# A second buffer for key and query parts, and a new order at the start of the first attention

## The chip, the cores and the metric

The kernel runs on one core of a Trainium2 chip. The metric is the device time in microseconds (us) of one execution, the median of several.

## What is computed

Two layers of cross-attention, each followed by a gated block, on `x` of shape (8, 256, 256) and a context `ctx_1024` of the same shape, in float32. The change touches the first of the four parts alone:

```python
# part 1: 16 heads of 16 columns; queries from the normed x, keys and values from the context
x = x + tanh(g_xattn[0]) * L0_xattn(_layernorm(x), ctx_1024, ctx_1024, Wq, bq, Wk, bk, Wv, bv, Wo, bo)
    # q = Q @ Wq + bq, k = K @ Wk + bk, v = V @ Wv + bv
    # out = softmax(q k^T / sqrt(16)) v, heads joined, @ Wo + bo
x = x + tanh(g_ffn[0]) * L0_ffn(_layernorm(x), ...)             # slots, routing, GRU
x = x + tanh(g_xattn[1]) * L1_xattn(ctx_1024, _layernorm(x), ...)  # 8 heads of 128
x = x + tanh(g_ffn[1]) * L1_ffn(x, ...)                         # quantized gate/up/down
```

## The kernel before

Each of the four parts is a function of its own with its own blocks of engine code, semaphores and a barrier at its end. `attention0` (line 91 on) is the first; a batch is one of 8 sequences of 256 positions. Each engine's instructions stand in the order in which the source issues them, and an engine executes its own list in that order; waits on semaphores tie the lists together. SP and, in places, ScalarE and POOL issue DMAs.

Precision is kept by splitting: each of context, normed x, weights, keys and queries is held as a high part (float32r) and a low part (the rest). For a batch `n`, TensorE transposes context and normed x (`ctxT`, `xnT`, L587), ScalarE copies the high part (`ctxT_hi`, `xnT_hi`, L327, L332), VectorE the low part (`ctxT_lo`, `xnT_lo`, L461, L465). `project_k` and `project_q` (L606) are 12 matmuls each into PSUM; `k_high`/`q_high` (L342, ScalarE) and `k_low`/`q_low` (L471, VectorE) write the parts into `k_parts` and `q_parts`, of which there is one buffer. From there 24 DMAs of 64 KB a batch (`place`, L180) put the rows high, high, low (queries) beside high, low, high (keys) into `q_stack` and `k_stack`, which have two buffers, by the batch's parity (`par`). Each stack has two halves: steps 0 to 3 of a batch read half 0, steps 4 to 7 half 1. Semaphores `stack0` and `stack1` count the copies of a half.

A batch has 8 steps `r`, each for two heads. `scores(b, par, r)` (L645, 4 matmuls) makes scores from the stacks for the maxima, which VectorE takes in `pair_max` (L494, 2 instructions); POOL splits a pair of maxima (`split_max`), TensorE turns them (`turn_max`, L668) and ScalarE copies them (`shift_out`, L361). `shifted_scores` (L658, L661) makes the scores again, transposed, less the maximum, ScalarE takes the exponentials (L356), and `group` (L679) multiplies with the values. The scores run 4 steps ahead of the shifted scores, and batch `b + 2` is projected while batch `b` is attended to. Batches 0 and 1 are prepared ahead of the loop by code written out by hand, at the end of each engine's block:

- SP: after the loads, `first_stacks()` waits in turn for `k_hi`, `k_lo`, `q_hi` and `q_lo` of batch 0 and issues 6 key copies and 4 query copies for half 0 and 6 query copies for half 1; then `load_ctx(2)`, the load of x 2, and `stacks(1, 1, False)`.
- POOL: after its constants and `rstd_of(1)`, waits for `k_lo` and issues the 6 key copies of half 1 (L299, semaphore `first`); then `split_max(0, 0)`.
- ScalarE: `k_high(0)`, `xnT_hi(0)`, `ctxT_hi(1)`, the high part of Wv, `q_high(0)`, then waits for `q_lo` and issues the last 2 query copies of half 0, then `xnT_hi(1)`, tanh of the gates, `k_high(1)`, `q_high(1)`, `shift_out(0, 0)`.
- VectorE: ..., `q_low(0)`, `v_out(0)`, `xnT_lo(1)`, `k_low(1)`, two `pair_max`, `q_low(1)`, two `pair_max`.
- TensorE: ..., `xnT(1)`, `project_k(1)`, `scores(0,0,0)`, `project_q(1)`, `scores(0,0,1)` to `scores(0,0,3)`, `turn_max(0,0)`, and then the loop with `shifted_scores(0,0,0)` first.

`high` makes `k_high(n)` and `q_high(n)` wait until all copies of batch `n - 1` have landed, since they read the one buffer that it writes:

```python
act.wait_ge(s[projected], n + 1)
wait(act, s["stack0"], HALF * n)
wait(act, s["stack1"], HALF * n - HALF // 2)
if isinstance(n, int) and n == 1:
    act.wait_ge(s["first"], HALF // 2)
```

Of the kernel before, what the change touches and what calls it, by code (L numbers as in the profile page):

```python
# [27 lines left out]
F32 = mybir.dt.float32  # L28
F32R = mybir.dt.float32r
# [3 lines left out]
P = 128  # L33
B, T, D = 8, 256, 256
# [46 lines left out]

def flat(ap):
    return ap.rearrange("p a d -> p (a d)")
# [16 lines left out]
def attention0(nc, a, x_sb, ident, gates, gru):  # L100
# [7 lines left out]
    with ctx:  # L108
# [21 lines left out]
        cT_lo = sb("a_cT_lo", [P, 2, DC * T], F32R)  # L130
        k_parts = sb("a_k_parts", [P, 2, DC * T], F32R)
        q_parts = sb("a_q_parts", [P, 2, DC * T], F32R)
        k_stack = sb("a_k_stack", [P, 2, NR, T], F32R)
# [20 lines left out]

        names = """bias x0 x1 x2 x ident ident0 first gate load_k load_q load_v load_b load_g load_o ctx next wk wq wv scale
                   const ones zeros mask pick stats moments var rstd xn cT cT_hi cT_lo xT xT_hi xT_lo k k_hi k_lo q q_hi
# [18 lines left out]

        def place(eng, parts, stack, which, half, par):

            for i, part in which:
                for e in range(HP):
                    eng.dma_start(stack[64 * e + DK * i:64 * e + DK * i + DK, par, 4 * half:4 * half + 4, :].bitcast(F32),  # L180
                                  parts[64 * e:64 * e + 64, part, half * T:(half + 1) * T].bitcast(F32)).then_inc(s[("stack0", "stack1")[half]], DMA)

# [3 lines left out]
        def _(sp):  # L186
# [8 lines left out]
            def stacks(n, par, again):  # L195
                for half in range(2):
                    if later(n):
                        pause(sp, s[("stack0", "stack1")[half]], HALF * n - half * HALF // 2, s["sp_passed"])
# [4 lines left out]
                    place(sp, k_parts, k_stack, K_ROWS, half, par)  # L203
                    if half == 0:
                        pause(sp, s["q_lo"], n + 1, s["sp_passed"])
                    place(sp, q_parts, q_stack, Q_ROWS, half, par)

# [4 lines left out]
            def first_stacks():  # L212

                sp.wait_ge(s["k_hi"], 1)
                place(sp, k_parts, k_stack, K_ROWS[:2], 0, 0)
                sp.wait_ge(s["k_lo"], 1)
                place(sp, k_parts, k_stack, K_ROWS[2:], 0, 0)
                sp.wait_ge(s["q_hi"], 1)
                place(sp, q_parts, q_stack, Q_ROWS[:2], 0, 0)
                sp.wait_ge(s["q_lo"], 1)  # L220
                place(sp, q_parts, q_stack, Q_ROWS, 1, 0)

# [37 lines left out]
        def _(pool):  # L260
# [33 lines left out]
            rstd_of(1)  # L294
            pool.wait_ge(s["zeros"], 1)
            pool.wait_ge(s["k_lo"], 1)
            for i, part in K_ROWS:
                for e in range(HP):
                    pool.dma_start(k_stack[64 * e + DK * i:64 * e + DK * i + DK, 0, 4:8, :].bitcast(F32),  # L299
                                   k_parts[64 * e:64 * e + 64, part, T:2 * T].bitcast(F32)).then_inc(s["first"], DMA)  # L300
            split_max(0, 0)
# [15 lines left out]
        def _(act):  # L317
# [16 lines left out]
            def high(n, projected, parts, bank, bias, done):  # L334

                act.wait_ge(s[projected], n + 1)
                wait(act, s["stack0"], HALF * n)
                wait(act, s["stack1"], HALF * n - HALF // 2)
                if isinstance(n, int) and n == 1:
                    act.wait_ge(s["first"], HALF // 2)  # L340
                for j in range(DC):
                    last = nc.scalar.activation(parts[:, 0, j * T:(j + 1) * T], bank[:, j * T:(j + 1) * T], ACT.Identity, bias=bias[:, j:j + 1])  # L342
                last.then_inc(s[done], 1)

            def k_high(n, bank=pK):
                high(n, "k", k_parts, bank, bkq[:, 0, :], "k_hi")

            def q_high(n, bank=pK):
                high(n, "q", q_parts, bank, bkq[:, 1, :], "q_hi")

# [23 lines left out]
            def batch(b, par, done, prep, more, old):  # L374
                for r in range(NR):
                    n, G = NR * b + r, 4 * b + r // 2
                    if r == 4 and prep:
                        k_high(b + 2)
                    if r == 6 and prep:
                        q_high(b + 2)  # L380
                    if r == 6 and done:
                        onT_out(b - 1)
                    if r == 1 and done:
                        group_out(b - 1, 1 - par, 3, True)
                    if r in (3, 5, 7):
                        group_out(b, par, r // 2 - 1, more or r < 7)
                    if r % 2 and (more or r < 7):
                        shift_out(G + 1, (r // 2 + 1) % 2)
                    exps(n, G, r)
                    if r == 1 and prep:  # L390
                        ctxT_hi(b + 2, par, pV)
                    if r == 3 and prep:
                        xnT_hi(b + 2, pV)
# [10 lines left out]
            act.wait_ge(s["bias"], 1)  # L404
            k_high(0, pK)
            xnT_hi(0, pP)
            ctxT_hi(1, 1, flat(pT[:, 0, :, :]))
            act.wait_ge(s["load_v"], 2 * DMA)
            nc.scalar.copy(w_hi[:, 2, :, :], w_raw[:, 2, :, :]).then_inc(s["wv"], 1)
            q_high(0, pV)  # L410
            act.wait_ge(s["q_lo"], 1)
            place(act, q_parts, q_stack, Q_ROWS[2:], 0, 0)
            xnT_hi(1, flat(pT[:, 1, :, :]))
            act.wait_ge(s["load_g"], 2 * DMA)
            nc.scalar.activation(gates[:, :], gates[:, :], ACT.Tanh).then_inc(s["gate"], 1)
            k_high(1, pP)
            q_high(1, pK)
            shift_out(0, 0)
# [5 lines left out]
        def _(dve):  # L424
# [49 lines left out]

            def k_low(n, bank=pK):
                low(n, "k_hi", k_parts, bank, bkq[:, 0, :], "k_lo")

            def q_low(n, bank=pK):
                low(n, "q_hi", q_parts, bank, bkq[:, 1, :], "q_lo")

# [37 lines left out]
            def batch(b, par, done, prep, more, old):  # L518
                for r in range(NR):
# [15 lines left out]
                    if r == 4 and prep:  # L535
                        xnT_lo(b + 2, pV)
                        k_low(b + 2)
                    if r == 5 and done:
                        divide(b - 1, 1)
                    if r == 6 and prep:  # L540
                        q_low(b + 2)
                    if r == 7 and old:
# [13 lines left out]
            norm_moments(1)  # L556
            k_low(0, pK)
            xnT_lo(0, pP)
# [3 lines left out]
            ctxT_lo(1, 1, flat(pT[:, 0, :, :]))  # L562
            q_low(0, pV)
            dve.wait_ge(s["ones"], 1)
            v_out(0, 0, pO[:, :, :].rearrange("p a t -> p (a t)"))
            xnT_lo(1, flat(pT[:, 1, :, :]))
            k_low(1, pP)
            pair_max(0, 0, 0)
            pair_max(1, 0, 1)
            q_low(1, pK)  # L570
            pair_max(2, 1, 2)
# [11 lines left out]
        def _(pe):  # L583
# [49 lines left out]
            def scores(b, par, r):  # L633
                n = NR * b + r
                wait(pe, s["max"], 2 * n)
                if r == 0:
                    pe.wait_ge(s["stack0"], HALF * b + HALF)
                if r == 4:
                    pe.wait_ge(s["stack1"], HALF * b + HALF // 2)
                if isinstance(b, int) and b == 0 and r == 4:  # L640
                    pe.wait_ge(s["first"], HALF // 2)
                for t in range(TT):
                    for e in range(HP):
                        rows = slice(64 * e, 64 * e + 3 * DK)
# [1636 lines left out]
```

## Time and profile before

| | |
|---|---|
| time, median of 3 runs | 954.78 us (954.57 to 954.9) |
| profiled execution, its own time | 955.44 us |
| its span, first to last instruction | 953.6 us |
| first attention | from 0 to about 216 us |
| busy over the span | TensorE 89%, VectorE 74%, ScalarE 53%, POOL 10% |
| granted TensorE clock, mean | 0.931 of full speed |

One execution was recorded by the profiler. Times are counted from the first instruction. A TensorE row gives matmuls; their ends are modelled, and they overlap. The granted clock is a share of 2.4 GHz: 1.00 is 2.4 GHz and 0.50 is 1.2 GHz. "Idle before" is the time in which an engine had nothing to run before the instruction, with the inferred releaser behind the arrow.

### The profile page before, as it was taken

The page shows a single profiled execution, that of the slowest core. Times are in us where ns is not written, and L with a number is a line of the kernel's source. Part 1 is how long each engine was busy: PE and PEld are TensorE (multiplying, and loading weights), DVE is VectorE, ACT ScalarE, POOL GpSimd, SP SyncE. Part 2 cuts the span into 40 slices and gives each one's busy share as a digit, 9 for nine tenths or more (in the row PEclk, how much of TensorE's full clock was granted, in tenths as well). Part 3 has the DMA queues.
Part 4 walks back from the last instruction along what each step waited for, and adds up shares of the span by engine and source line. Part 5 has one row for each costly group of instructions (what it writes and reads, how often), then busy time and mean ns, then how long its engine had stood idle before and what let it go on. Part 6 is the DMA issues. An engine that isn't in the chain of part 4 may idle for free. (4 is left out here: it accounts for less than half of the span.)

```text
span 953.6 us, 16759 instructions
## 1 busy us (share of the span) xinstructions
PE 846.5 (89%) x5559; PEld 677.7 (71%) x5559; DVE 704.8 (74%) x1588; ACT 505.9 (53%) x1068; POOL 98.9 (10%) x166
## 2 busy tenths in 40 slices
PE   4799999986577389999999999999899999998767
PEld 4677777654345268888888878888788888886323
DVE  4578878735665658888788778797688787875586
ACT  3366666642343146556556546556455555554764
POOL 3010010000400000010000000000000000000456
PEclk9599999996768799999999999999999999999887
DMA  7332222405000410000000000000000000000002
GB/s 145 110 110 91 98 97 68 150 1 189 0 1 0 101 53 12 1 1 12 1 12 1 1 14 1 1 12 1 3 12 1 1 1 2 1 1 1 1 1 89
DMA packets 37857, 33.33 MB, mean 35 GB/s; under 512 B 10225, under 2 KB 36529, under 8 KB 37521
## 3 DMA queue, kind: packets, MB, share of 16 engines
q1 hardware_dynamic: 37424, 31.76, 11.0%
q8 instruction: 47, 0.77, 0.4%
q0 software_dynamic: 192, 0.39, 0.3%
q10 hardware_dynamic: 160, 0.13, 0.1%
q14 instruction: 34, 0.27, 0.1%
HBM read 17.59 MB, written 2.10 MB: 21 GB/s over the span
## 5 line engine op out<-in xcount | busy, mean ns | idle before, releaser
L1410 ACT ACTIVATE c_probs<-c_pS,c_neg_max 128x512 f32<-128x512 f32 x128 | 88.2, 689 | 113.9 <-DVE c_neg_max L1554 113.9
L1554 DVE TENSOR_REDUCE c_neg_max<-c_pS 128x1 f32<-128x512 f32 x128 | 88.3, 690 | 66.7 <-PE c_pS L1811 64.8
L494 DVE TENSOR_REDUCE a_neg_max<-a_pS 128x2 f32<-128x512 f32 x128 | 82.4, 686 | 17.2 <-PE a_pS L645 16.7
L1549 DVE TENSOR_TENSOR c_pT_lo<-c_pT,c_pT_hi 128x512 fp32r<-128x512 f32 x128 | 87.1, 681 | 3.2 <-ACT c_pT_hi L1418 3.2
L356 ACT ACTIVATE a_probsT<-a_pT 128x512 f32<-128x512 f32 x128 | 69.6, 597 | 33.9 <-PE a_pT L661 33.0
L1828 PE MATMUL c_pO<-c_pT_hi,c_v_hi 128*128 128x256 f32 x256 | 77.5, 303 | 3.1 <-DVE c_pT_lo L1549 3.1
L1818 PE MATMUL c_pT<-ident,c_probs 128*128 128x128 f32 x512 | 77.4, 274 | 0.3 <-DVE c_probs L1561 0.3
L1818 PEld LDWEIGHTS c_pT<-ident,c_probs 128*128 128x128 f32 x512 | 64.3, 142 | 18.3 <-DVE c_probs L1561 0.8
L1418 ACT CAST c_pT_hi<-c_pT 128x512 fp32r<-128x512 f32 x128 | 74.0, 579 | 0.0
L1828 PE MATMUL c_pO<-c_pT_hi,c_v_lo 128*128 128x256 f32 x256 | 72.0, 281 | 0.0
L1828 PE MATMUL c_pO<-c_pT_lo,c_v_hi 128*128 128x256 f32 x256 | 72.0, 281 | 0.0
L1423 ACT ACTIVATE c_oT<-c_pO,c_bv 128x256 f32<-128x256 f32 x64 | 30.4, 475 | 76.5 <-PE c_pO L1828 74.1
L1811 PE MATMUL c_pS<-c_k_hi,c_q_hi 128*128 128x512 f32 x128 | 64.0, 500 | 4.7 <-issue 4.7
L1838 PE MATMUL c_pX<-c_wo,c_oT 128*128 128x256 f32 x256 | 65.8, 380 | 1.2 <-ACT c_oT L1423 1.2
L1561 DVE TENSOR_SCALAR c_probs<-c_probs,c_r_sum 128x512 f32<-128x512 f32 x128 | 63.3, 495 | 4.5
L1772 PE MATMUL c_pK<-c_kv_hi,w_hi 128*128 128x512 f32 x128 | 52.4, 409 | 4.8 <-DVE c_kv_lo L1529 3.9
L1798 PE MATMUL c_pK<-w_hi,c_kv_hi 128*128 128x512 f32 x124 | 50.7, 409 | 2.2 <-DVE c_k_lo L1533 2.2
L1533 DVE SCALAR_TENSOR_TENSOR c_k_lo<-c_pK,c_bk,c_k_hi 128x512 fp32r<-128x512 f32 x64 | 47.7, 746 | 6.3 <-ACT c_k_hi L1392 6.3
L1772 PE MATMUL c_pK<-c_kv_hi,w_lo 128*128 128x512 f32 x128 | 52.1, 407 | 0.0
L1772 PE MATMUL c_pK<-c_kv_lo,w_hi 128*128 128x512 f32 x128 | 52.0, 406 | 0.0
L1828 PEld LDWEIGHTS c_pO<-c_pT_hi,c_v_hi 128*128 128x128 f32 x256 | 48.2, 188 | 4.2 <-DVE c_pT_lo L1549 4.2
L1811 PE MATMUL c_pS<-c_k_hi,c_q_lo 128*128 128x512 f32 x128 | 50.6, 395 | 0.0
(372 smaller groups left out, 2177.0 us busy)
## 6 DMA issues: line engine op xcount, KB each, us to landing
a_q_stack<-a_q_parts SPq DMA_DIRECT2D x94, 64.0 KB, 2.6
a_k_stack<-a_k_parts SPq DMA_DIRECT2D x90, 64.0 KB, 2.6
a_ctx_in<-in_ctx_dram SPq DMA_DIRECT2D x8, 256.0 KB, 2.7
x_sb<-in_x_dram SPq DMA_DIRECT2D x8, 256.0 KB, 3.1
b_raw<-in_L_xattn_Wkv_dram SPq DMA_DIRECT2D x1, 2048.0 KB, 11.2
ctx_in<-in_ctx_dram SPq DMA_DIRECT2D x8, 256.0 KB, 2.7
out_dram<-x_sb SPq DMA_DIRECT2D x8, 256.0 KB, 2.2
b_raw<-in_L_xattn_Wq_dram SPq DMA_DIRECT2D x1, 1024.0 KB, 6.8
```

Source lines behind the costliest of these rows:

```text
L356: nc.scalar.activation(probsT[:, r // 2 % 2, 2 * (r % 2) + e, :, :], pT[:, e, :, :], ACT.Exp).then_inc(s["exp"], 1)
L494: nc.vector.tensor_reduce(neg_max[:, r // 2 % 2, :, e, r % 2], pS[:, e, :, :], AX_X, ALU.max, negate=True).then_inc(s["max"], 1)
L1410: nc.scalar.activation(probs[:, u % 2, :], pS[:, u % 2, :], ACT.Exp, bias=neg_max[:, u % 4:u % 4 + 1], accum_out=sums[:, u % 4:u % 4 + 1]) ...
L1418: nc.scalar.copy(pT_hi[:, u // 2 % 2, :, half], pT[:, u % 2, :].rearrange("p (t q) -> p t q", q=P)).then_inc(s["T_hi"], 1)
L1549: nc.vector.tensor_tensor(pT_lo[:, u // 2 % 2, :, half], pT[:, u % 2, :].rearrange("p (t q) -> p t q", q=P), pT_hi[:, u // 2 % 2, :, half] ...
L1554: nc.vector.tensor_reduce(neg_max[:, u % 4:u % 4 + 1], pS[:, u % 2, :], AX_X, ALU.max, negate=True).then_inc(s["max"], 1)
L1561: nc.vector.tensor_scalar(probs[:, u % 2, :], probs[:, u % 2, :], r_sum[:, u % 4:u % 4 + 1], None, ALU.mult).then_inc(s["probs"], 1)
L1772: last = nc.tensor.matmul(pK[:, :], W[x][:, c, INNER + h * DH:INNER + (h + 1) * DH], KV[y][:, par, c, :], start=(c == 0 and i == 0), stop= ...
L1811: last = nc.tensor.matmul(pS[:, u % 2, :], (q_hi, q_lo)[x][:, slot, qs], (k_hi, k_lo)[y][:, slot, :], start=(i == 0), stop=(i == 2))
L1818: last = nc.tensor.transpose(pT[:, u % 2, t * P:(t + 1) * P], probs[:, u % 2, t * P:(t + 1) * P], ident[:, :])
L1828: last = nc.tensor.matmul(pO[:, 0:T], (v_hi, v_lo)[x][:, h // 4, t, (h % 4) * DH:(h % 4 + 1) * DH], (pT_hi, pT_lo)[y][:, h % 2, t, :], sta ...
L1838: last = nc.tensor.matmul(pX[:, t, :], oT[:, h % 2, t * P:(t + 1) * P], wo[:, h, :], start=(h == 0 and t == 0), stop=(h == H1 - 1), skip_g ...
```

## The change

`k_parts` and `q_parts` get a second buffer, chosen by the batch's parity, so `high` waits for the copies of batch `n - 2`. On TensorE `project_q(1)` goes ahead of `scores(0,0,0)`, and `turn_max(0,0)` ahead of `scores(0,0,3)`. On VectorE `q_low(1)` goes ahead of the first `pair_max`. ScalarE issues no copies any more; POOL issues these two (waiting for `q_lo`) and then its six key copies. ScalarE's tanh goes behind `q_high(1)`. The semaphore `first` becomes `first_q` and `first_k`, and the counts of `stack0` are adapted. The core of the diff:

```diff
-        k_parts = sb("a_k_parts", [P, 2, DC * T], F32R)
-        q_parts = sb("a_q_parts", [P, 2, DC * T], F32R)
+        k_parts = sb("a_k_parts", [P, 2, 2, DC * T], F32R)
+        q_parts = sb("a_q_parts", [P, 2, 2, DC * T], F32R)
...
-        def place(eng, parts, stack, which, half, par):
+        def place(eng, parts, stack, which, half, par, done):
...
-                                  parts[64 * e:64 * e + 64, part, half * T:(half + 1) * T].bitcast(F32)).then_inc(s[("stack0", "stack1")[half]], DMA)
+                                  parts[64 * e:64 * e + 64, par, part, half * T:(half + 1) * T].bitcast(F32)).then_inc(done, DMA)
...
             pool.wait_ge(s["zeros"], 1)
+            pool.wait_ge(s["q_lo"], 1)
+            place(pool, q_parts, q_stack, Q_ROWS[2:], 0, 0, s["first_q"])
             pool.wait_ge(s["k_lo"], 1)
-            for i, part in K_ROWS:
-                for e in range(HP):
-                    pool.dma_start(k_stack[64 * e + DK * i:64 * e + DK * i + DK, 0, 4:8, :].bitcast(F32),
-                                   k_parts[64 * e:64 * e + 64, part, T:2 * T].bitcast(F32)).then_inc(s["first"], DMA)
+            place(pool, k_parts, k_stack, K_ROWS, 1, 0, s["first_k"])
...
-                wait(act, s["stack0"], HALF * n)
-                wait(act, s["stack1"], HALF * n - HALF // 2)
-                if isinstance(n, int) and n == 1:
-                    act.wait_ge(s["first"], HALF // 2)
+                wait(act, s["stack0"], HALF * (n - 1) - 2 * DMA)
+                wait(act, s["stack1"], HALF * (n - 1) - HALF // 2)
+                if isinstance(n, int) and n == 2:
+                    act.wait_ge(s["first_k"], 6 * DMA)
+                    act.wait_ge(s["first_q"], 2 * DMA)
...
-            q_high(0, pV)
-            act.wait_ge(s["q_lo"], 1)
-            place(act, q_parts, q_stack, Q_ROWS[2:], 0, 0)
+            q_high(0, 0, pV)
             xnT_hi(1, flat(pT[:, 1, :, :]))
+            k_high(1, 1, pP)
+            q_high(1, 1, pK)
             act.wait_ge(s["load_g"], 2 * DMA)
             nc.scalar.activation(gates[:, :], gates[:, :], ACT.Tanh).then_inc(s["gate"], 1)
-            k_high(1, pP)
-            q_high(1, pK)
             shift_out(0, 0)
...
-            k_low(1, pP)
+            k_low(1, 1, pP)
+            q_low(1, 1, pK)
             pair_max(0, 0, 0)
             pair_max(1, 0, 1)
-            q_low(1, pK)
             pair_max(2, 1, 2)
...
                 if r == 0:
-                    pe.wait_ge(s["stack0"], HALF * b + HALF)
+                    pe.wait_ge(s["stack0"], HALF * b + HALF - 2 * DMA)
...
-                if isinstance(b, int) and b == 0 and r == 4:
-                    pe.wait_ge(s["first"], HALF // 2)
+                if isinstance(b, int) and b == 0 and r in (0, 4):
+                    pe.wait_ge(s[("first_q", "first_k")[r // 4]], (2, 6)[r // 4] * DMA)
...
             project_k(1, 1, pP, (s["xT_lo"], 1))
+            project_q(1, pK, (s["k_lo"], 1))
             scores(0, 0, 0)
-            project_q(1, pK, (s["k_lo"], 1))
             scores(0, 0, 1)
             scores(0, 0, 2)
             pe.wait_ge(s["pick"], 1)
             pe.wait_ge(s["vb"], 1)
+            turn_max(0, 0)
             scores(0, 0, 3)
-            turn_max(0, 0)
```

## Rows read from the trace of the kernel before

**Rows 1.** Windows: stretch, its length, busy time per engine, granted clock, DMA share, GB/s

```profile
22.00:24.00 2.00, 0.29 (x2) 0.29 (x4) 0.00 (x0) 0.00 (x0) 0.00 (x0) 0.79 1.17 147
80.00:102.00 22.00, 22.00 (x234) 16.72 (x233) 18.02 (x38) 14.30 (x31) 2.28 (x9) 1.00 0.30 97
```

**Rows 2.** Timeline, TensorE: start, duration, instruction, count, idle before and releaser

```profile
16.75 0.60 PE L587 MATMUL a_pT<-ident,a_xn 128*128 128x128 f32 x4
...
23.71 0.80 PE L645 MATMUL a_pS<-a_k_stack,a_q_stack 48*128 48x256 f32 x4 [4.94 <-DMA a_q_stack<-a_q_parts]
...
33.59 0.80 PE L645 MATMUL a_pS<-a_k_stack,a_q_stack 48*128 48x256 f32 x4 [1.48 <-DVE a_neg_max L494]
...
35.56 0.58 PE L658 MATMUL a_pT<-a_q_stack,a_k_stack 48*128 48x256 f32 x2 [0.55 <-ACT a_shift L361]
...
36.55 0.66 PE L645 MATMUL a_pS<-a_k_stack,a_q_stack 48*128 48x256 f32 x4
...
43.88 0.40 PE L645 MATMUL a_pS<-a_k_stack,a_q_stack 48*128 48x256 f32 x4
```

**Rows 3.** Timeline, VectorE, first 36 us

```profile
12.26 0.88 DVE L471 SCALAR_TENSOR_TENSOR a_k_parts<-a_pK,a_bkq,a_k_parts 128x256 fp32r<-128x256 f32 x2 [0.75 <-ACT a_k_parts L342]
...
16.40 0.88 DVE L471 SCALAR_TENSOR_TENSOR a_q_parts<-a_pV,a_bkq,a_q_parts 128x256 fp32r<-128x256 f32 x2 [0.82 <-ACT a_q_parts L342]
...
27.01 0.88 DVE L471 SCALAR_TENSOR_TENSOR a_k_parts<-a_pP,a_bkq,a_k_parts 128x256 fp32r<-128x256 f32 x2 [6.96 <-ACT a_k_parts L342]
27.80 1.28 DVE L494 TENSOR_REDUCE a_neg_max<-a_pS 128x2 f32<-128x512 f32 x2
29.97 1.29 DVE L494 TENSOR_REDUCE a_neg_max<-a_pS 128x2 f32<-128x512 f32 x2 [0.89 <-PE a_pS L645]
```

**Rows 4.** Timeline, ScalarE (ACTq is its DMA issues), first 30 us

```profile
17.31 1.33 ACTq L180 DMA_DIRECT2D a_q_stack<-a_q_parts  x2
18.74 0.59 ACT L332 CAST a_xT_hi<-a_pT 128x512 fp32r<-128x512 f32 x1 [2.37 <-issue]
...
26.13 0.84 ACT L342 ACTIVATE a_k_parts<-a_pP,a_bkq 128x256 fp32r<-128x256 f32 x2 [6.70 <-DMA a_q_stack<-a_q_parts]
```

**Rows 5.** Landing of L180 (SP, ScalarE) from 10 to 30 us, then of L299 (POOL)

```profile
DMA to landing us min/median/max: 2.5/4.2/5.4
...
DMA to landing us min/median/max: 3.2/3.7/4.3
```

**Rows 6.** Timeline, issues of SP and POOL: start, time of all issues together, count

```profile
16.39 6.42 SPq L180 DMA_DIRECT2D a_q_stack<-a_q_parts  x10
22.93 0.52 SPq L193 DMA_DIRECT2D a_ctx_in<-in_ctx_dram  x1
...
27.98 3.74 SPq L180 DMA_DIRECT2D a_k_stack<-a_k_parts  x6
...
50.50 4.22 SPq L180 DMA_DIRECT2D a_k_stack<-a_k_parts  x6
...
13.80 3.27 POOL L299 DMA_DIRECT2D a_k_stack<-a_k_parts  x6 [1.51 <-DVE a_k_parts L471]
```

**Rows 7.** Windows of L606 alone: busy time of TensorE and weight load, granted clock, DMA

```profile
17.00:19.00 2.00, 1.67 (x12) 1.49 (x12) 1.00 1.14 148
24.00:28.00 4.00, 2.93 (x12) 2.63 (x12) 0.50 0.69 147
```

**Rows 8.** Timeline, ScalarE, steps 3 and 6 of batches 1 and 2

```profile
67.39 1.09 ACT L356 ACTIVATE a_probsT<-a_pT 128x512 f32<-128x512 f32 x2 [0.41 <-PE a_pT L661]
...
70.21 0.84 ACT L342 ACTIVATE a_k_parts<-a_pK,a_bkq 128x256 fp32r<-128x256 f32 x2 [1.26 <-DMA a_q_stack<-a_q_parts]
...
76.57 1.11 ACT L356 ACTIVATE a_probsT<-a_pT 128x512 f32<-128x512 f32 x2
...
90.28 1.09 ACT L356 ACTIVATE a_probsT<-a_pT 128x512 f32<-128x512 f32 x2 [0.47 <-PE a_pT L661]
...
98.65 1.10 ACT L356 ACTIVATE a_probsT<-a_pT 128x512 f32<-128x512 f32 x2
```

More of the change, by code:

```diff
@@ L153, in attention0 @@
         pV = pb("a_pV", [P, 512])
-        names = """bias x0 x1 x2 x ident ident0 first gate load_k load_q load_v load_b load_g load_o ctx next wk wq wv scale
+        names = """bias x0 x1 x2 x ident ident0 first_k first_q gate load_k load_q load_v load_b load_g load_o ctx next wk wq wv scale
                    const ones zeros mask pick stats moments var rstd xn cT cT_hi cT_lo xT xT_hi xT_lo k k_hi k_lo q q_hi
@@ L197, in stacks @@
                     if later(n):
-                        pause(sp, s[("stack0", "stack1")[half]], HALF * n - half * HALF // 2, s["sp_passed"])
+                        pause(sp, s[("stack0", "stack1")[half]], HALF * n - (2 * DMA, HALF // 2)[half], s["sp_passed"])
                     if again:
@@ L202, in stacks @@
                         pause(sp, s["k_lo"], n + 1, s["sp_passed"])
-                    place(sp, k_parts, k_stack, K_ROWS, half, par)
+                    place(sp, k_parts, k_stack, K_ROWS, half, par, s[("stack0", "stack1")[half]])
                     if half == 0:
                         pause(sp, s["q_lo"], n + 1, s["sp_passed"])
-                    place(sp, q_parts, q_stack, Q_ROWS, half, par)
+                    place(sp, q_parts, q_stack, Q_ROWS, half, par, s[("stack0", "stack1")[half]])
             def load_x(n):
@@ L214, in first_stacks @@
                 sp.wait_ge(s["k_hi"], 1)
-                place(sp, k_parts, k_stack, K_ROWS[:2], 0, 0)
+                place(sp, k_parts, k_stack, K_ROWS[:2], 0, 0, s["stack0"])
                 sp.wait_ge(s["k_lo"], 1)
-                place(sp, k_parts, k_stack, K_ROWS[2:], 0, 0)
+                place(sp, k_parts, k_stack, K_ROWS[2:], 0, 0, s["stack0"])
                 sp.wait_ge(s["q_hi"], 1)
-                place(sp, q_parts, q_stack, Q_ROWS[:2], 0, 0)
+                place(sp, q_parts, q_stack, Q_ROWS[:2], 0, 0, s["stack0"])
                 sp.wait_ge(s["q_lo"], 1)
-                place(sp, q_parts, q_stack, Q_ROWS, 1, 0)
+                place(sp, q_parts, q_stack, Q_ROWS, 1, 0, s["stack1"])
             load_ctx(0)
@@ L343, in high, with k_high, q_high @@
                 last.then_inc(s[done], 1)
[L345 to L349, printed above, removed]
+            def k_high(n, par, bank=pK):
+                high(n, "k", k_parts[:, par, :, :], bank, bkq[:, 0, :], "k_hi")
+            def q_high(n, par, bank=pK):
+                high(n, "q", q_parts[:, par, :, :], bank, bkq[:, 1, :], "q_hi")
             def exps(n, G, r):
@@ L377, in batch @@
                     if r == 4 and prep:
-                        k_high(b + 2)
+                        k_high(b + 2, par)
                     if r == 6 and prep:
-                        q_high(b + 2)
+                        q_high(b + 2, par)
                     if r == 6 and done:
@@ L404, in _ @@
             act.wait_ge(s["bias"], 1)
-            k_high(0, pK)
+            k_high(0, 0, pK)
             xnT_hi(0, pP)
@@ L473, in low, with k_low, q_low @@
                 last.then_inc(s[done], 1)
[L475 to L479, printed above, removed]
+            def k_low(n, par, bank=pK):
+                low(n, "k_hi", k_parts[:, par, :, :], bank, bkq[:, 0, :], "k_lo")
+            def q_low(n, par, bank=pK):
+                low(n, "q_hi", q_parts[:, par, :, :], bank, bkq[:, 1, :], "q_lo")
             def v_out(n, par, bank=pK):
@@ L536, in batch @@
                         xnT_lo(b + 2, pV)
-                        k_low(b + 2)
+                        k_low(b + 2, par)
                     if r == 5 and done:
@@ L540, in batch @@
                     if r == 6 and prep:
-                        q_low(b + 2)
+                        q_low(b + 2, par)
                     if r == 7 and old:
@@ L556, in _ @@
             norm_moments(1)
-            k_low(0, pK)
+            k_low(0, 0, pK)
             xnT_lo(0, pP)
@@ L562, in _ @@
             ctxT_lo(1, 1, flat(pT[:, 0, :, :]))
-            q_low(0, pV)
+            q_low(0, 0, pV)
             dve.wait_ge(s["ones"], 1)
```

## The prediction

> **What bounds the kernel now.** I read four views, in this order. The windows of all engines first: in the middle of the first attention TensorE is busy for the whole of a stretch of 22 us, which is one batch, so a step there is only worth something if TensorE was kept waiting [rows 1]. Then the timelines of TensorE, VectorE and ScalarE over the first 75 us, side by side, because the change moves work there. TensorE ends the key projection of batch 1 at 18.8 us and starts nothing until 23.71 us, where `scores(0,0,0)` waits for a DMA into `q_stack`; twelve us later, at 35.56 us, comes the first shifted score, and from there on it is busy [rows 2]. The reader is to see that the scores are not what is late in those twelve us. VectorE could have taken the first maxima at 24.5 us and takes them at 27.80, because `k_low(1)` stands ahead of them in its queue and waited 6.96 us for `k_high(1)` [rows 3]. And `k_high(1)` on ScalarE waited 6.70 us for DMAs out of `q_parts`: with one buffer of parts, batch 1 may not be written until all 24 copies of batch 0 have been read [rows 4]. So the start is a chain: copies of batch 0 landed, `k_high(1)`, `k_low(1)`, first maximum, three more rounds of scores and maxima, shift, first shifted score. Last the DMA views: the copies land after 2.5 to 5.4 us in this stretch [rows 5]; the issues themselves run at 0.64 us each on SP [rows 6].
>
> **The change part by part.** Two buffers of `k_parts` and `q_parts` take the wait away from `k_high(1)`. `project_q(1)`, `q_high(1)` and `q_low(1)` are put ahead of the scores and the first maxima. ScalarE loses its two issues, which stand between `q_high(0)` and `xnT_hi(1)`; POOL makes them ahead of its six key copies, which thereby wait for `q_low(0)` instead of `k_low(0)`. `turn_max(0,0)` goes ahead of `scores(0,0,3)`.
>
> Projections of batch 1. ScalarE spent 17.31 to 18.64 us issuing and began `xnT_hi(1)` at 18.74 [rows 4], though TensorE had its input ready at 17.35 [rows 2]. After the change it begins at 17.45 and ends 0.59 us later, at 18.05; `xnT_lo(1)`, about 0.7 us, ends at 18.75; `project_q(1)` follows `project_k(1)` at 18.85 and takes the 1.67 us that twelve such matmuls took at the higher clock, to 20.5 [rows 7]. On the other side `k_high(1)` runs from 18.9 to 19.7 (0.84 us [rows 4]), `k_low(1)` to 20.6 (0.88 us [rows 3]), `q_high(1)` to 21.45 and `q_low(1)` to 22.35. All of it lies in the time in which TensorE now waits for the stacks. If that cover were gone, the first maximum would wait for 22.35 us.
>
> First scores. They need SP's four high query copies and POOL's two low ones. SP's start at 16.39 us, 0.64 us apart (6.42 us for ten), so the fourth starts at 18.3 us [rows 6]; at 3.2 us to landing it is there at 21.5. The old time, 23.71, fits this fourth copy at the largest landing of the stretch, 5.4 us (18.3 + 5.4 = 23.7) [rows 5]: it was slowed by POOL's six key copies, in flight from 13.80 us on [rows 6], which now come behind. POOL began 0.66 us after `k_low(0)` ended at 13.14 [rows 3, 6]. `q_low(0)` ends at 17.28 us [rows 3], so POOL starts at 17.95 and its second copy at 18.7. The trace has no low query copy on POOL; the nearest rows are its own six, 3.2, 3.7 and 4.3 us at least, median and most, and on the other side the 5.4 us of the crowded SP and ScalarE queues [rows 5]. I take 3.7, as these copies are of the same size and queue: `scores(0,0,0)` at 22.4 us, between 21.9 and 24.1. The clock fell in the pause before 23.71 (granted 0.79 of full speed, 2.4 GHz, over 22 to 24 us, and the scores took 0.80 us where they take 0.40 later) [rows 1, 2]. The pause is now 1.9 us long instead of 4.9, so I take 2.4 GHz for the first two scores and 1.2 GHz behind them: the first maximum at 22.85 us, the second 2.17 - 0.40 us later (27.80 to 29.97 [rows 3]) at 24.6, the third at 26.8.
>
> A rule of the Trainium skill speaks against moving these two copies: the page "DMA: Bandwidth & Descriptors" (section "Latency and other measured facts") puts the first byte of a DMA issued by GpSimd at about 1 us and of one issued by Sync or Scalar at about 0.6 us. The case's landings run the other way, 3.7 us on POOL and 4.2 us on SP and ScalarE together, because what is in flight counts for more [rows 5]. By the page alone the sum below would be 0.4 us smaller.
>
> First shifted score. `scores(0,0,3)` waits for the third maximum (26.8 + 1.29) and starts at 28.2 us. Before, the shifted score came 1.97 us after it, with turn and shift in between [rows 2]; these now lie beside the third maximum, so it comes after the 0.75 us of the scores, at 28.95. Then a new wait: `scores(0,0,4)` needs the fourth maximum, 29.05 to 30.35 us, and so starts at 30.45 instead of following at once (it came 0.99 us behind before). From 36.55 to 30.45 us are 6.1 us gained [rows 2]. `scores(0,0,4)` also needs POOL's six key copies: issued from 19.2 to 22.5 us (3.27 us for six [rows 6]) and landed after 5.4 us at most, by 28, so 2 us of cover. The wait for `q_low(0)` that they stand behind holds nothing else, as POOL's next step, `split_max(0,0)`, needs the second maximum at 25.9.
>
> Batch 1. `k_high(3)` waited 1.26 us for DMAs out of `q_parts`; this occurs once, as from batch 2 on the copies are done in time. From the exponentials of step 3 to those of step 6 batch 1 took 76.57 - 67.39 = 9.18 us and batch 2 took 98.65 - 90.28 = 8.37 us [rows 8]. The other buffer takes away the wait: 0.8 us, with 0 as the other bound (the wait may have been covered by batch 1's other gaps). Nothing else changes in the loops: same instructions, same counts. The buffers' room and the strides cost nothing.
>
> Sum: 6.1 + 0.8 = 6.9 us. The profiled execution took 955.44 us (span 953.6), so it would take 948.5. Its time stands 0.66 us above the median of 954.78, which becomes 947.9.
>
> **The rivals.**
> *Crowded landing.* POOL's two copies meet SP's queue, and `scores(0,0,0)` comes at 24.1 us (5.4 us to landing [rows 5]). 1.7 us are lost, and 0.8 us for two scores at 1.2 GHz: 947.9 + 2.5 = 950.4. For it: before, every copy behind POOL's took 4 us or more. Against: ahead of POOL's two there is now one queue that issues every 0.64 us. The page named above (section "Queues, rings and completion order") says that each DMA engine takes turns between its queues; that would give POOL's copies a share even in the crowd, and supports the shorter landing.
> *Clock kept.* With `project_q(1)` in the pause and the scores closer together, the clock never falls. Two more scores at 0.40 us less, and `project_v(1)` in 1.67 us instead of 2.93 [rows 7] in the stretch up to 43 us, which was at 1.2 GHz: 2.1 us more gained, 945.8. Against: between the scores TensorE still stands idle more than half of the time.
> *SP's queue becomes the bound.* SP's list moves up less than the computation: `stacks(1)` starts when its query copies and two loads are issued, at 24.0 instead of 27.98, 4.0 us [rows 6]. If it sets the pace of batch 1, the gain is 4.0: 950.8. Against: 24 issues of 0.64 us and four loads from 27.98 on end near 45.4, and the next copies start at 50.50 only, behind `k_low(2)` [rows 6], 5 us of slack.
> *Nothing gained.* The start is given back to something later, such as a load of the next stage, and the time stays 954.8. No wait for a DMA shows there.
> *Slower.* One mechanism: the clock. 2.9 us of matmuls leave the stretch of 24 to 28 us, and if TensorE's thin work at the start leaves it at 1.2 GHz deep into the dense part, the batches run slow. Each projection then costs 2.93 instead of 1.67 us, 1.26 us [rows 7]; the gain of 6.9 is used up at 6 projections, two whole batches, and a third makes it 956 or more. Before, 2.4 GHz was back by 43.88 us, 8 us after the dense work began [rows 2].
>
> **How the numbers follow.** Forecast 0.50, crowded landing 0.18, clock kept 0.17, SP 0.07, nothing gained 0.04, slower 0.04. The likeliest time is 947.9, with 946.9 to 949 as its own range. The overall range goes down to clock kept (945.8) and one projection's 1.26 us more, for the clock's steps fall elsewhere in all later stages: 944.5. Up it goes to the SP case and to the crowded one with batch 1's 0.8 us not gained: 951.3. What a measurement can tell from no change is 0.2%, 1.9 us; faster 0.92, same 0.04, slower 0.04.
>
> **What would show it.** In the changed profile: `k_high(1)` at 18.9 us with no wait for a DMA; `scores(0,0,0)` near 22.4 and the first maximum near 22.85, not behind `k_low(1)`; the first shifted score at 28.95 and `scores(0,0,4)` at 30.45 with a wait for VectorE; no DMA wait before `k_high(3)` and batch 1's steps as long as batch 2's. The distance to the old trace should be 6 us at batch 0, 6.9 from batch 2 on, and the same at the end. The prediction is wrong if the distance shrinks in the later stages, if POOL's copies land after 24 us, or if the first scores still last 0.80 us.

## The result

The changed kernel took 948.59 us (median of 4 executions, 946.31 to 950.58) against 954.84 (4, 954.57 to 955.45): a ratio of 0.9936 with a 95% interval of 0.9919 to 0.9952. The forecast was 947.9. On a second chip it was 948.81 us against 954.30, ratio 0.9931 (0.9915 to 0.9947); one of the old kernel's 23 executions there fell in the chip's slow state (1008.31 us, granted clock 0.813) and is left out of the ratio.

### The profile after

The profiled execution took 946.31 us, span 944.5, at the quick end of its four; so its distance to the old one, 9.1 us, must not be read as the change's effect without looking where it arises. The timeline of TensorE over the start answers to [rows 2]:

```profile
18.95 0.38 PE L604 MATMUL a_pK<-a_xT_hi,a_w_hi 128*128 128x256 f32 x1
...
22.13 0.50 PE L643 MATMUL a_pS<-a_k_stack,a_q_stack 48*128 48x256 f32 x4 [1.50 <-DMA a_q_stack<-a_q_parts]
24.01 0.80 PE L643 MATMUL a_pS<-a_k_stack,a_q_stack 48*128 48x256 f32 x4 [1.39 <-DVE a_neg_max L492]
26.19 0.80 PE L643 MATMUL a_pS<-a_k_stack,a_q_stack 48*128 48x256 f32 x4 [1.38 <-DVE a_neg_max L492]
26.93 0.68 PE L666 MATMUL a_pO<-ident,a_max_parts 128*128 128x128 f32 x2
28.38 0.80 PE L643 MATMUL a_pS<-a_k_stack,a_q_stack 48*128 48x256 f32 x4 [0.77 <-DVE a_neg_max L492]
28.97 0.42 PE L656 MATMUL a_pT<-a_q_stack,a_k_stack 48*128 48x256 f32 x2
...
30.56 0.80 PE L643 MATMUL a_pS<-a_k_stack,a_q_stack 48*128 48x256 f32 x4 [0.53 <-DVE a_neg_max L492]
```

`project_q(1)` now begins at 18.95 us, in the old pause. The first shifted score (L656) comes at 28.97 instead of 35.56, and `scores(0,0,4)` at 30.56 instead of 36.55, with the wait for VectorE that was forecast. ScalarE and VectorE over the same stretch, answering to [rows 3, 4]:

```profile
17.58 0.59 ACT L331 CAST a_xT_hi<-a_pT 128x512 fp32r<-128x512 f32 x1 [1.01 <-PE a_pT L585]
19.01 0.84 ACT L342 ACTIVATE a_k_parts<-a_pP,a_bkq 128x256 fp32r<-128x256 f32 x2 [0.84 <-PE a_pP L604]
```

```profile
21.54 0.88 DVE L469 SCALAR_TENSOR_TENSOR a_q_parts<-a_pK,a_bkq,a_q_parts 128x256 fp32r<-128x256 f32 x2 [0.77 <-ACT a_q_parts L342]
22.67 1.29 DVE L492 TENSOR_REDUCE a_neg_max<-a_pS 128x2 f32<-128x512 f32 x2 [0.26 <-PE a_pS L643]
```

`k_high(1)` starts 7.1 us earlier and waits for TensorE, no longer for a DMA; the first maximum follows at 22.67 us behind `q_low(1)`, with 0.26 us to spare. Steps 3 and 6 of batch 1 answer to [rows 8]:

```profile
61.29 1.09 ACT L356 ACTIVATE a_probsT<-a_pT 128x512 f32<-128x512 f32 x2 [0.41 <-PE a_pT L659]
...
63.14 0.84 ACT L342 ACTIVATE a_k_parts<-a_pK,a_bkq 128x256 fp32r<-128x256 f32 x2 [0.29 <-PE a_pK L604]
...
69.58 1.10 ACT L356 ACTIVATE a_probsT<-a_pT 128x512 f32<-128x512 f32 x2
```

They are 8.29 us apart (9.18 before), and `k_high(3)` waits for TensorE. Batch 2 starts its exponentials at 74.71 us against 81.71: 7.0 us. That distance still stands at the last exponentials of the first attention (195.97 against 202.95). What comes on top, 2.1 us, arises later; the experiments return to it.

### The profile page after: what moved, and what is told of

Same layout as the page of the kernel before. It is cut to its first block and busy times, and to the rows that moved or that the text cites. A ratio compares the mean times of both kernels' runs of the same rounds, so it can differ in the third digit from the quotient of the medians.

```text
span 944.5 us, 16756 instructions
## 1 busy us (share of the span) xinstructions
PE 839.1 (89%) x5557; PEld 671.5 (71%) x5559; DVE 706.1 (75%) x1588; ACT 506.3 (54%) x1068; POOL 100.0 (11%) x168
```

## The experiments

Theory A: the wait for the single buffer of parts carried the start, and buffer and order together give 6 to 7 us by batch 2, which are kept. Its rivals: the order alone gains, or the buffer alone; it does not matter who issues. Theory C: the granted clock makes the rest. The experiments ran on several chips, so each ratio is to the kernel before on the same chip, and stages are compared in the traces, mostly with the changed kernel's second profile.

### The changed kernel again

The kernel unchanged, to see its spread on another chip.

> The changed kernel again, beside the kernel before on one chip. Theory A (the gain is made by 75 us and kept): ratio 0.993, 948 us, and in every run the first exponentials of batch 2 start 7.0 us earlier than before (74.7 against 81.7 us). The four known times spread from 946.3 to 950.6 us where those of before spread over 0.9 us; theory C (the clock): the spread comes with the mean granted clock, 0.946 at 944.5 us span down to 0.936 at 948.8, and is made behind the first attention. Against C: were the spread made in the first attention, batch 2 would start at another time in a run with another total.

Measured: 948.81 us (6 executions, 947.11 to 950.01), ratio 0.9931 (0.9915 to 0.9947). Batch 2 starts at 74.78 us, 0.07 us from the other profile of the same kernel, although the spans differ by 2.9 us (947.4 and 944.5). The spread thus arises behind the first attention. Two stretches in which they differ, from the windows of the quicker profile and then of this one (length, busy time by engine, granted clock, DMA share, GB/s):

```profile
677.00:690.00 13.00, 10.17 (x62) 8.66 (x61) 8.42 (x21) 5.02 (x12) 0.00 (x0) 1.00 0.02 6
866.00:944.50 78.50, 54.10 (x278) 26.79 (x280) 53.10 (x92) 44.76 (x75) 37.52 (x36) 0.87 0.08 27
```

```profile
677.00:690.00 13.00, 10.36 (x54) 8.74 (x52) 7.15 (x17) 5.11 (x13) 0.00 (x0) 0.87 0.02 6
868.00:947.00 79.00, 56.85 (x280) 28.25 (x280) 51.71 (x92) 44.45 (x75) 37.20 (x36) 0.82 0.08 27
```

Near 681 us TensorE stood still for 2.35 us in the quicker one and for 2.64 us in the other; in the quicker one the clock stayed at 1.00, in the other it fell, and fewer matmuls (54 against 62) were done in the same 13 us. A stretch near 545 us was likewise shorter in the quicker one, 2.03 against 2.59 us. Matching the maxima of the third part in the two traces, the distance is 0.09 us up to the first of these stretches, 0.7 behind it, 0.97 at the second and 1.9 when the clock is back; the last 1.1 us arise in the fourth part.

### One buffer, all else as changed

```diff
-        k_parts = sb("a_k_parts", [P, 2, 2, DC * T], F32R)
+        k_parts = sb("a_k_parts", [P, 1, 2, DC * T], F32R)
...
-                wait(act, s["stack0"], HALF * (n - 1) - 2 * DMA)
-                wait(act, s["stack1"], HALF * (n - 1) - HALF // 2)
-                if isinstance(n, int) and n == 2:
+                wait(act, s["stack0"], HALF * n - 2 * DMA)
+                wait(act, s["stack1"], HALF * n - HALF // 2)
+                if isinstance(n, int) and n == 1:
```

(`q_parts` likewise, and `par` becomes 0 where the parts are addressed.)

> The changed order with one buffer of parts: k_high(1) waits for all 24 copies of batch 0 again. Theory A (that wait carried the start): k_high(1) at 26 to 27 us, since the last of SP's copies lands there, q_low(1) follows by 28.7, so the first maximum comes at 28.8 us, 6.1 us later than with two buffers, and k_high(3) waits 1.3 us again: 948.6 + 6.1 + 0.8 = 955.5, no faster than before. Rival B (the new order is what gained, the buffer little): the first maximum stays before 25 us and the time stays under 951.

Measured: 956.82 us (953.64 to 960.28, 10 executions), ratio to the kernel before 1.0024 (1.0008 to 1.0040): all of the gain is gone, and the kernel is even slightly slower than before. Batch 2 starts at 83.17 us, 1.5 us behind the kernel before. ScalarE's timeline:

```profile
27.90 0.84 ACT L342 ACTIVATE a_k_parts<-a_pP,a_bkq 128x256 fp32r<-128x256 f32 x2 [9.88 <-DMA a_q_stack<-a_q_parts]
```

The wait is back, longer than in the kernel before, since the copies start later and land after up to 5.8 us. The first maximum comes at 30.35 us, 1.5 us later than expected. The expected wait at `k_high(3)` did not come (it waited 0.29 us for TensorE): batch 1 had been held up earlier, where the granted clock fell to 0.51 between 60 and 63 us. That part of the expectation could not be judged here; the run after next does it. Rival B (the order alone) falls.

### The kernel before with two buffers alone

Its edit is the first four lines of the change's diff and the waits for batch `n - 2`; order and issuers as before.

> The kernel before with the second buffer of parts alone; order and issuers as before. Theory A (buffer and order are needed together): k_high(1) at 19 us, but project_q(1) stands between scores 0 and 1 and costs 2.9 us at 1.2 GHz, so the first shifted score comes at 33.8 us and scores(0,0,4) at 34.8 instead of 36.55: 1.75 us, and 0.8 us in batch 1, 952.3. Rival B (the buffer alone brings it): near 948.6.

Measured: 951.47 us (949.18 to 955.09, 10 executions), ratio 0.9971 (0.9954 to 0.9987). `scores(0,0,4)` starts at 35.00 us (expected 34.8), batch 2 at 78.55, 3.2 us before the old kernel. The timeline of TensorE shows why the buffer alone does not do it: `project_q(1)` fills the time between scores 0 and 1, which are 3.6 us apart.

```profile
24.00 0.80 PE L645 MATMUL a_pS<-a_k_stack,a_q_stack 48*128 48x256 f32 x4 [5.06 <-DMA a_q_stack<-a_q_parts]
...
27.58 0.79 PE L645 MATMUL a_pS<-a_k_stack,a_q_stack 48*128 48x256 f32 x4
```

By the start of batch 2 the buffer alone gives 3.2 us of the 7.0, and order and issuers on top of it the other 3.8. Order and issuers without the buffer lose 1.5 us (the run before).

### The old wait from batch 3 on

```diff
-                wait(act, s["stack0"], HALF * (n - 1) - 2 * DMA)
-                wait(act, s["stack1"], HALF * (n - 1) - HALF // 2)
+                late = 0 if not isinstance(n, int) or n > 2 else 1
+                wait(act, s["stack0"], HALF * (n - late) - 2 * DMA)
+                wait(act, s["stack1"], HALF * (n - late) - HALF // 2)
```

> As changed, but from batch 3 on k_high and q_high wait for the copies of the batch before again. Theory A: k_high(3) waits for SP's copies and batch 1 grows by 0.8 us, batches 2 to 5 not: 949.4; batch 2's first exponentials at 75.5 instead of 74.7 us. Rival B: batch 1's extra length was hidden by its other gaps, nothing moves.

Measured: 949.37 us (948.11 to 952.19). The total cannot tell 0.8 us from none, the trace can: `k_high(3)` waits 1.32 us for the copies, and batch 2 starts at 75.68 us instead of 74.78 (the changed kernel's second profile), 0.9 us later, though batch 1 started at the same time (52.62 against 52.68). Batch 3 follows 22.07 us behind, as in the changed kernel. The term of batch 1 is right in size and place.

```profile
64.21 0.84 ACT L343 ACTIVATE a_k_parts<-a_pK,a_bkq 128x256 fp32r<-128x256 f32 x2 [1.32 <-DMA a_q_stack<-a_q_parts]
```

### Who issues, and the crowd

Two kernels. The first undoes the move of issues: ScalarE issues the two low query copies, POOL its key copies right behind `k_low(0)`.

```diff
-            pool.wait_ge(s["q_lo"], 1)
-            place(pool, q_parts, q_stack, Q_ROWS[2:], 0, 0, s["first_q"])
...
             q_high(0, 0, pV)
+            act.wait_ge(s["q_lo"], 1)
+            place(act, q_parts, q_stack, Q_ROWS[2:], 0, 0, s["first_q"])
             xnT_hi(1, flat(pT[:, 1, :, :]))
```

> Two buffers and the new order, but ScalarE issues the two low query copies and POOL its six key copies right behind k_low(0), as before. Theory A: scores(0,0,0) is held by SP's copies in the crowd, at 23.7 us instead of 22.1, and q_low(1) ends at 23.7, so the first maximum comes at 24.5 and all is 1.8 us later: 950.4. Rival B (who issues does not matter): the first scores stay near 22.1 and the time within 0.5 us of the changed kernel's.

Measured: 950.38 us (947.96 to 953.63, 10 executions), ratio 0.9955 (0.9939 to 0.9970); `scores(0,0,0)` at 24.05 us, the first maximum at 24.60, batch 2 at 76.73 against 74.78: 1.95 us.

The second lets ScalarE issue, but keeps POOL's key copies behind `q_low(0)` (the `pool.wait_ge(s["q_lo"], 1)` stays).

> As changed, but ScalarE issues the two low query copies; POOL's key copies stay behind q_low(0). It parts the crowd from the issuer. If the crowd of POOL's early key copies is what slowed the landing, scores(0,0,0) starts at 21 to 22 us, no later than as changed. But xnT_hi(1) is 1.3 us later behind the issues, q_low(1) ends at 23.7, and the first maximum comes at 23.7 instead of 22.7: 949.5, 1 us slower. If the issuer is what matters, scores(0,0,0) starts after 23 us here too.

Measured: 949.22 us (948.68 to 949.60). `scores(0,0,0)` starts at 22.32 us: with the key copies kept back, the landing is short though ScalarE issues. This run and the one before it differ only in when POOL issues its key copies (from 18.14 us, and from 14.11), so it was the crowd and not the issuer. In the window of 16 to 20 us of this run ScalarE's two copies landed after 3.2 us (first line); on POOL, in the changed kernel, the same two took 2.9 us (18 to 20 us, the other lines):

```profile
a_q_stack<-a_q_parts ACTq DMA_DIRECT2D x2, 64.0 KB, 3.2
...
a_q_stack<-a_q_parts SPq DMA_DIRECT2D x4, 64.0 KB, 3.5
a_q_stack<-a_q_parts POOLq DMA_DIRECT2D x2, 64.0 KB, 2.9
a_k_stack<-a_k_parts POOLq DMA_DIRECT2D x2, 64.0 KB, 4.2
```

So the first-byte rule weighed in the prediction (the Trainium skill, "DMA: Bandwidth & Descriptors", section "Latency and other measured facts": GpSimd's DMAs slower by 0.4 us) is not to be seen in these landings, 0.3 us the other way. The pair is not clean, though: POOL's key copies were issued from 18.14 us on beside ScalarE's two, and in the changed kernel only from 19.38 us on, behind POOL's two. The rest of the expectation missed: the first maximum did come 1 us later, at 23.69 us, as worked out, but batch 2 started at 74.87 us, only 0.09 us behind. Part of the reason is in the timeline: two scores at 0.50 us instead of one, the clock having fallen later, where the changed kernel has 0.80 from its second on. That gives back 0.3 us; `scores(0,0,4)` still starts 0.74 us behind (31.28 against 30.54). The rest came back behind it, beside a clock that rose earlier (granted 0.86 over 36 to 38 us against 0.64 in the changed kernel's second profile).

```profile
22.32 0.50 PE L644 MATMUL a_pS<-a_k_stack,a_q_stack 48*128 48x256 f32 x4 [0.34 <-DMA a_q_stack<-a_q_parts]
25.02 0.50 PE L644 MATMUL a_pS<-a_k_stack,a_q_stack 48*128 48x256 f32 x4 [2.20 <-DVE a_neg_max L493]
```

### The turn of the maxima behind the fourth scores again

```diff
-            turn_max(0, 0)
             scores(0, 0, 3)
+            turn_max(0, 0)
```

> As changed, but turn_max(0,0) behind scores(0,0,3) again. Theory A: turn and shift come between scores(0,0,3), 28.4 us, and the first shifted score, which starts at 30.3 instead of 28.97. But scores(0,0,4) waits for the fourth maximum until 30.5 in any case, and now follows the shifted scores at 31.3: 0.8 us later, and 0.8 us on the total (949.4). Rival B (the wait for the fourth maximum hides it): no difference at batch 1.

Measured: 950.19 us (948.87 to 950.49). The first shifted score moves to 30.59 us and `scores(0,0,4)` to 31.59, 1.0 us later than in the changed kernel's second profile; but at batch 1 only 0.22 us are left (52.90 against 52.68), and 0.24 at batch 2. Of these, 0.18 us were there before the edit could act: `scores(0,0,0)` started at 22.29 us against 22.11. The granted clock came back a little earlier (0.81 against 0.64 over 36 to 38 us), and the delay was given back beside it. Theory A holds at batch 0, where the move saves 0.9 us; at batch 1 nothing clear of such offsets is left, as rival B had it, though not for its reason. The total, 1.4 us higher, came from the later parts, where the spread is that large.

### Fillers: is it the clock?

Thirty-two matmuls whose result nobody reads are put into TensorE's gaps.

```diff
+            def fill(count):
+                for _ in range(count):
+                    nc.tensor.matmul(pT[:, 0, 0, :], w_hi[:, 0, 0, 0:P], xT_hi[:, 0:T], start=True, stop=True)
+
             project_q(1, pK, (s["k_lo"], 1))
+            fill(8)
             scores(0, 0, 0)
+            fill(9)
             scores(0, 0, 1)
+            fill(9)
             scores(0, 0, 2)
             pe.wait_ge(s["pick"], 1)
             pe.wait_ge(s["vb"], 1)
             turn_max(0, 0)
+            fill(6)
             scores(0, 0, 3)
```

> As changed, with 32 matmuls more whose result nobody reads, in TensorE's idle gaps: 8 before scores 0, 9 behind it, 9 behind scores 1, 6 before scores 3, 0.12 us each at 2.4 GHz. Theory C (the low clock costs 2 us between 23 and 37 us): the granted clock stays 1.00 there, the scores last 0.40 us, project_v(1) 1.6 us, and batch 2 starts 2 us earlier, at 72.7 us: 946.6. Rival: the clock is not limiting there, since VectorE's maxima set the pace, or the fillers fall into 1.2 GHz and delay the scores: no gain, or up to 2 us lost.

Measured: 943.96 us (941.48 to 944.80), ratio 0.9888 (0.9872 to 0.9905): 5 us better than the changed kernel, but not where expected. The clock did stay at 1.00 to 33 us, the scores took 0.50 us, and the first exponentials came at 28.84 us; then batch 1 began at 53.27, later than without fillers (52.68). VectorE names the new last comer:

```profile
31.78 0.75 DVE L437 BATCH_NORM_STATS2 a_stats<-x_sb 128x6 f32<-128x256 f32 x2 [2.13 <-DMA x_sb<-in_x_dram]
```

The load of x 2, issued behind all first copies, took 8.1 us to land, from 23.58 us. VectorE's wait kept `scores(0,0,5)` from starting (TensorE idle 2.7 us), the clock fell after all, and `project_v(1)` ran at 1.2 GHz. In both profiles of the changed kernel x 2, issued at the same time, landed after 5.7 us, at 29.2 us, 1.2 us before it was asked for. With such a landing VectorE, free near 29.6 us in the filler kernel, would not have waited either: it was the longer landing and not the faster start alone. Long landings go with the fillers (ctx 2 took 6.7 us here and 7.5 us in the next run, 5.2 to 5.5 us in the changed kernel and its near relatives); their cause was not looked for.

Next, the same with the load of x 2 ahead of `first_stacks()`, where SP was idle:

> The kernel with 32 fillers in the gaps of the start, and the load of x 2 issued ahead of the first stacks, at 8.5 us, instead of behind them at 23.6. In the filler run the granted clock stayed 1.00 to 33 us, the first exponentials came 1.2 us earlier (28.84), and then VectorE waited 2.13 us for x 2, which landed after 8.1 us in the crowd of copies; batch 1 began at 53.27 instead of 52.59 us. Theory: without that wait the clock's gain is kept, batch 1 begins 1.2 to 2 us before the changed kernel's, at 50.6 to 51.4, and the total is 2 to 2.7 us under the filler run's 944: 941.5. Rival: the loads of ctx 2 (6.7 us to landing in the filler run) or the clock take its place and batch 1 begins at 52.6 or later.

Measured: 939.80 us (939.33 to 942.92), ratio 0.9848 (0.9820 to 0.9877), the fastest kernel of the study and faster than expected. The windows show the granted clock at 1.00 through the start:

```profile
24.00:27.00 3.00, 2.53 (x20) 2.02 (x21) 1.80 (x4) 0.00 (x0) 0.40 (x2) 1.00 1.14 148
27.00:30.00 3.00, 2.05 (x24) 1.65 (x22) 2.40 (x6) 1.46 (x3) 0.11 (x1) 1.00 1.03 182
...
33.00:36.00 3.00, 3.00 (x40) 2.33 (x38) 2.70 (x6) 1.79 (x4) 0.39 (x2) 1.00 0.34 111
```

Batch 1 starts at 49.66 us (expected 50.6 to 51.4) and batch 2 at 71.77, 3.0 us before the changed kernel. That is what the low clock still cost in it; 2.1 us had been put down for this in the rival "clock kept". The next limit already shows: TensorE waits 0.41 us for the load of ctx 2. Moving the load of x 2 alone must tell whether the load has a part of its own:

> As changed, with the load of x 2 ahead of the first stacks and no fillers. Theory: in the changed kernel x 2 lands at 29.2 us and VectorE asks for it at 30.4, so there is 1.2 us of cover and nothing to gain while the scores run at 1.2 GHz: batch 2 at 74.7 us, time 948.6 to 949. Rival: the load's 256 KB less in the crowd bring the stacks or ctx 2 earlier, and batch 2 starts before 74.2 us.

Measured: 948.46 us (948.04 to 948.96), ratio 0.9945 (0.9926 to 0.9964); batch 2 at 74.64 us, 0.14 us earlier. The load's cover was enough as long as the clock was low; it is the second limit behind the first.

### Where the other five microseconds of the fillers came from

Between its first and last maximum the third part takes 524.4 us in the filler kernel, 530.4 and 532.1 in the two profiles of the changed one and 531.3 in the kernel before. Two stretches in which TensorE stands still make 4.4 of the 6.0 us between the filler kernel and the first profile. First of the kernel before, then of the changed one:

```profile
551.71 0.47 PE L1811 MATMUL c_pS<-c_k_hi,c_q_hi 128*128 128x512 f32 x1 [2.01 <-issue]
...
687.99 0.47 PE L1811 MATMUL c_pS<-c_k_hi,c_q_hi 128*128 128x512 f32 x1 [2.65 <-issue]
```

```profile
544.62 0.47 PE L1809 MATMUL c_pS<-c_k_hi,c_q_hi 128*128 128x512 f32 x1 [2.03 <-issue]
...
680.75 0.47 PE L1809 MATMUL c_pS<-c_k_hi,c_q_hi 128*128 128x512 f32 x1 [2.35 <-issue]
```

At the same two places TensorE waits for nothing that the profile shows, and about the stretch of 540 to 546 us the DMA view lists only queues of kind "instruction":

```profile
q8 instruction: 2, 0.03, 2.2%
q14 instruction: 2, 0.02, 1.0%
```

The filler kernel has no idle stretch of "issue" there. Theory D: what matters is where TensorE's later instructions lie. So the same number of matmuls goes to the end of the first attention, behind the last `out_project`, where it can do nothing for the start; once in the changed kernel, once in the one before:

```diff
             out_project(B - 1)
+            for _ in range(32):
+                nc.tensor.matmul(pT[0:32, 0, 0, 0:64], w_hi[:, 0, 0, 0:32], xT_hi[:, 0:64], start=True, stop=True)
```

> As changed, with 32 small matmuls more, whose result nobody reads, behind the last out_project of the first attention, where TensorE waits for the other engines anyway. The kernel with 32 fillers at the start gained 5 us, but not in the first attention: TensorE's two idle stretches of 2.0 and 2.4 us before c_k_hi x c_q_hi at 544 and 681 us, put down to issue, are gone in it. Theory D (where TensorE's later instructions lie decides on these stalls): they vanish here too, the third part takes 525 us instead of 531 between its first and last maximum, and the total falls to 943.5. Theory C (they went because the clock stood higher at the start): nothing changes behind the first attention, 948.8 to 949.

Measured: 942.31 us (941.36 to 943.52), ratio 0.9863 (0.9837 to 0.9888), 6.5 us under the changed kernel on its second chip. The two stretches are gone and the third part takes 524.3 us. Batch 2 starts at 74.28 us, 0.5 us earlier than in the changed kernel's second profile, though nothing differs ahead of it: differences of that size at batch 2 say little.

> The kernel before with the same 32 small matmuls at the end of its first attention. Theory D: the stalls at 552 and 688 us vanish, 954.5 becomes 949, with no change at the start at all. Theory C: 954.5 to 955.

Measured: 947.86 us (946.45 to 948.57) against 955.17, ratio 0.9925 (0.9902 to 0.9948): 7.3 us, with nothing changed at its start (batch 2 at 81.74 us against 81.71). The third part takes 524.4 us. Theory D stands, and the clock as their cause falls. The traces show what else changed. Packets of the instruction queue q8 over 520 to 780 us, in the changed kernel and then with the matmuls at the end of the first attention:

```profile
q8 instruction: 17, 0.28, 0.4%
...
q8 instruction: 1, 0.02, 0.0%
```

Over the whole span q8 moves 47 packets (0.77 MB) in each of the ten traces that have the two stretches, and 29 (0.48 MB) in each of the four that have not. So with the 32 matmuls the loop of the third part runs almost without loading instructions, and without them it takes in a packet of 16 KB about every 15 us. That TensorE stood still for want of instructions is thus likely, but it remains argued: most of these packets have no idle stretch beside them, and how the stretches depend on the number of instructions added was not tried.

## Why the prediction was right

Point by point. **What bounds** was read rightly: with one buffer everything was lost, with the wait gone `k_high(1)` started at 19.0 us (forecast 18.9). **The projections** lay in TensorE's pause as worked out; `q_low(1)` ended at 22.42 us, forecast 22.35. **The first scores** came at 22.13 us, forecast 22.4: the term for landing was too large for POOL's copies (2.7 and 3.1 us measured, 3.7 taken), and POOL started 0.2 us later than said. That the crowd and not the issuer made the old landing was argued in the prediction and shown by the two issuer runs. **The clock** was put at 2.4 GHz for two scores; it held for one (0.50, then 0.80 us). And a score behind a pause takes 0.50 us at a granted clock of 1.00, not the 0.40 of the dense stretch that the sum used, so a score at the higher clock is worth 0.3 us here and not 0.4. By luck the misses cancelled within 0.2 us: the third maximum came at 27.03 us, forecast 26.8. **The first shifted score and the new wait**: 28.97 and 30.56 us, forecast 28.95 and 30.45; the gain there was 6.0 us against 6.1. **Batch 1**: 0.9 us by the steps of the profile (9.18 less 8.29) and 0.9 us in the run with the old wait, against 0.8. At batch 2 the distance was 7.0 us, forecast 6.9, and it was kept to the end of the first attention.

The medians lie 6.25 us apart, 0.65 us less than the 6.9. This is inside what the later parts spread over (946.3 to 950.6 us with equal starts), so no term of the sum is to blame; on the second chip the distance is 5.5 us. In the first profile the later parts added 2.1 us, in the second they took 0.8 away (947.4 us of span, 6.2 below the old one). The prediction had named a distance that shrinks in the later stages as a sign of being wrong; it shrank in the second profile, but by less than the 2.9 us by which two profiles of the same kernel differ there, so the sign was too strict. That the total came within 0.7 us of the forecast is in this sense luck; what bears the prediction out are the times up to batch 2.

**The rivals.** The crowded landing did not happen, since the key copies went behind. (Not every copy behind POOL's took 4 us or more before, as the prediction says: SP's three issued between 13.9 and 15 us landed after 3.2 us, median.) The clock was not kept, but what it would be worth was underpriced: 3.0 us measured at batch 2 against 2.1. SP's queue never became the bound, but it was nearer than the prediction's 5 us of slack: in the kernel before, its last load was issued by 46.8 us and the next copies at 50.50, 3.7 us later; in the changed kernel at 43.0 and 44.40, 1.4 us later, behind `k_low(2)`. The prediction did not name two things. The load of x 2 sits behind the crowd and had only 1.2 us of cover in the changed kernel; in the filler run, where it landed 2.4 us later, the start's gain was given back to it. And the third part holds two stretches that hang on TensorE's instruction list, worth as much as the whole change; they stand in both kernels, since the change reorders TensorE's matmuls and adds none (q8 moves 47 packets in both).

## What to carry to other kernels

Look for the engine whose queue has a long wait ahead of work that is already due: here the maxima stood 3.3 us behind a projection part that waited for copies to be read, and it took both a second buffer and a new order to free them fully. When a start gets faster, list the loads behind the crowd of copies with their landing times, since one of them may be the next to be late. And before a small gain or loss is credited to an edit, compare the same stage in both traces: a kernel with a few more instructions can move by 7 us somewhere else.

## What the hardware showed that was not expected

Thirty-two matmuls of no use, at a place where TensorE waits anyway, made two idle stretches of 2.0 to 2.65 us vanish 330 and 470 us later, and the kernels 6.5 and 7.3 us faster (0.7%); the packets of the instruction queue q8 fell from 47 to 29 with them. Equal programs with starts equal to 0.07 us differ by 2.9 us at the end: 0.9 us of it by the two stretches being longer in one, 0.9 beside a granted clock that fell behind the second of them in one and not in the other, and the rest in the fourth part. Filling TensorE's gaps with unread matmuls held the granted clock at 1.00 and was worth 3.0 us at the second batch, once the next load in line had been moved.
